# Four tiles of K ahead of the first V, and K's first half behind half of the weight fold, in a linear-attention and feed-forward kernel on eight cores

## The chip, the cores and the metric

The kernel runs on the 8 NeuronCores of one Trainium2 chip, each with 4 of the 32 sequences and no exchange between cores. The metric is the device time in microseconds of the slowest core.

## The reference

One layer on x of shape 32 x 2048 x 1024 in float32, cut to what matters:

```python
def attn(x):                      # 16 heads of 64
    Q, K, V = heads(x @ Wq.T + bq), heads(x @ Wk.T + bk), heads(x @ Wv.T + bv)
    Qf = relu(Q * 64**-0.25 @ P.T) + 1e-6
    Kf = relu(K * 64**-0.25 @ P.T) + 1e-6
    KV, Ksum = einsum('bhnf,bhnd->bhfd', Kf, V), Kf.sum(axis=2)
    out = einsum('bhnf,bhfd->bhnd', Qf, KV) / (einsum('bhnf,bhf->bhn', Qf, Ksum) + 1e-6)[..., None]
    return merge_heads(out) @ Wo.T + bo

def ffn(x):                       # 1024 -> 4096 -> 1024
    h = fix8(x @ w1 + b1)         # fix8 rounds to multiples of 2**-8
    h = fix8(piecewise_linear_gelu(h))
    return fix8(h @ w2 + b2)

x = x + layernorm(attn(layernorm(x)))
x = x + layernorm(ffn(layernorm(x)))
```

## The kernel before

A core's 4 sequences are 64 tiles of 128 rows. The first stage (the loop over `t`, line 778) reads each tile of x once. DVE takes its statistics (`ln_stats`, `ln_aggr`), POOL raises the variance to the power -1/2, DVE applies both (`ln_apply`, writes `xn`), PE transposes the tile in eight pieces (`ln_transpose`) and DVE copies the result out of PSUM into `xnT` (`ln_evac`); from tile 8 on a DMA transposes instead. Then `k_proj` (16 matmuls of 512 columns in two halves into banks 0 and 1, and after each half an add on DVE into `kf`), `k_floor` (the maximum with 1e-6 on DVE), `v_proj` (16 matmuls into banks 2 and 3, copied out by ACT into `vt`), and one tile later `kv_acc`, eight matmuls that add K'V into banks 5 to 7. From tile 3 on each step has two Q projections too (`q_proj`, evacuated by ACT, stored to DRAM).

The feature matrix P is folded into Wk and Wq on the chip. Wk comes in four pieces of 1 MB (`load_w`), each is cast to bf16, one half by DVE and one by ACT (`cast_w`), and `fold` multiplies it with P, 32 small matmuls for each half of the output columns, eight evacuations of 512 columns that ACT and DVE take in turn. The fold's first half needs pieces 0 and 1 alone, its second half pieces 2 and 3. Wv is cast and not folded. Wq is folded in the same way at t = 3, behind `v_proj(3)`, once it has been loaded into the place that Wk's float32 copy had.

All later stages (the chunks of M = KV Wo, the attention output, and the feed-forward part, by blocks of 256 rows) follow behind tile 63 and are not touched.

Order: nothing is scheduled by a tool. Each helper appends its instruction to the list of its engine, and an engine executes its list in the order in which the Python code ran; a helper's waits are semaphores that are worked out from the tokens (`t_...`) given to it. SP (`"Y"`) issues all loads of this stretch, in its written order too. Before the change SP issues: small constants, x tile 0, Wk in four pieces, x tile 1, Wv in four pieces, x tiles 2 and 3, then tiles 4 and 5 (each waits until `ln_apply` has read the tile four before it, whose buffer it takes), small constants, `sel`, and Wq in four pieces.

Work of the first tiles before the change, in the order of the text: LN and transposes of tile 0; fold of Wk, first and second half; statistics and apply of tile 1; `k_proj(0)`; transposes of tile 1; casts of Wv; `k_proj(1)`; `v_proj(0)`; floors; statistics of 2 and 3; apply of 2 and 3; transposes of 2; then for t = 1, 2, 3: `v_proj(t)`, statistics of t+4, apply of t+3, `kv_acc(t-1)`, transposes of t+2, with `k_proj(t)` at the head of each step from t = 2 on.

Lines that the steps name: casts L225 (DVE) and L226 (ACT), statistics L255 and L256, their aggregation L260, POOL's two L262 and L265, apply L271, transposes L283, evacuation L291, fold L311 with evacuations L318 (ACT) and L320 (DVE), K matmuls L371 and add L376, floor L383, V matmuls L389 and copy L394, Q matmuls L402, kv L421. DMAs have the line of the helper, L88.

Of the kernel before, what the change touches and what calls it, by code (L numbers as in the profile page):

```python
# [95 lines left out]
def build_program():  # L96
# [32 lines left out]
    with es:  # L129
# [4 lines left out]
        def sb(name, kb, cols, dt):  # L134
# [17 lines left out]
        xnT = [sb(f"xnT{i}", 148 + 8 * i, 8 * 512, BF16).rearrange("p (c j) -> p c j", j=512)  # L152
               for i in range(2)]
        kf = [sb(f"kf{i}", 164 + 2 * i, D, BF16) for i in range(2)]
        vt = [sb(f"vt{i}", 168 + 2080 * i / KB, 8 * 130, BF16).rearrange("p (c j) -> p c j", j=130)
              for i in range(2)]
        qst = [sb(f"qst{i}", 172.25 + i, 512, BF16) for i in range(4)]
# [71 lines left out]
            t_c0 = p.dma("Y", "c0", out, src)  # L229
        t_x[0] = p.dma("Y", "x0", xr[0], xtile[0])  # L230
        t_wk = [load_w("lk", k, wkf, wk_n) for k in range(4)]
        t_x[1] = p.dma("Y", "x1", xr[1], xtile[1])
        t_wv = [load_w("lv", k, wvf, wv_t) for k in range(4)]
        for t in range(2, 4):
            t_x[t] = p.dma("Y", f"x{t}", xr[t], xtile[t])

        t_one = p.V(lambda v: v.memset(one, 1.0))
        t_z = p.V(lambda v: v.memset(sel, 0.0))
        for col, val in ((c_half, -0.5), (c_q, 0.25), (c_seg, -31.5 / 64.0), (c_mag, MAGIC)):
            t_cst = p.V(lambda v, col=col, val=val: v.memset(col, val))  # L240
        for i in range(2):
# [34 lines left out]
        def load_x(t):  # L276
            t_x[t] = p.dma("Y", f"x{t % 4}", xr[t % 4], xtile[t], t_xn[t - 4])
# [27 lines left out]
        def fold(name, hf, src, dst, banks, t_src, ev):  # L305
            for d in range(8):
                n = hf * 8 + d
                i = banks[n % len(banks)]
                for c in range(4):
                    o = (hf * 4 + c) * D + d * 128  # L310
                    tt = p.T(lambda e, o=o, c=c, i=i: e.matmul(  # L311
                        bk[i][:, c * 128:c * 128 + 128], lhsT=src[:, o:o + 128], rhs=pbb,
                        start=(c == 0), stop=(c == 3)),
                        *((*t_src[4 * hf:4 * hf + 4], t_pbb, *t_free.get(i, ())) if c == 0 else ()),
                        sig=(c == 3))
                out = dst[:, d * D + hf * 512:d * D + hf * 512 + 512]
                if ev[n % len(ev)] == "S":
                    t_free[i] = [p.S(lambda s, out=out, i=i: s.copy(out=out, in_=bk[i]), tt)]  # L318
                else:
                    t_free[i] = [p.V(lambda v, out=out, i=i: v.tensor_copy(out=out, in_=bk[i]), tt)]  # L320
                t_fe[name] = [*t_fe.get(name, ())[-1:], *t_free[i]]
            return tt

        t_free = {}
# [17 lines left out]
        ln_evac(0)  # L342
        t_wkc += cast_w(2, stk, wkf, t_wk[2])
        fold("k", 0, stk, wkp, (0, 1, 2, 3), t_wkc, "SV")
        t_wkc += cast_w(3, stk, wkf, t_wk[3])
        t_fk = fold("k", 1, stk, wkp, (0, 1, 2, 3), t_wkc, "SV")
        ln_aggr(1, *ln_stats(1))
        ln_apply(1)
        for t in range(4, 6):
            load_x(t)  # L350
        for out, src in ((b1s, b1_d), (mskb, mskb_d), (msk16, msk16_d.rearrange("p (c j) -> p c j", j=16))):
            t_c1 = p.dma("Y", "c1", out, src)
        t_sel = p.dma("Y", "c2", sel[0:48], sel_d, t_z)
        t_wq = [load_w("lq", k, wqf, wq_n, *t_wkc[2 * k:2 * k + 2]) for k in range(4)]


        def centre_bo(t_in):
# [7 lines left out]

        t_ka, t_kf, t_ve, t_qe, t_kv, t_kve, t_qs = {}, {}, {}, {}, {}, {}, {}

        def k_proj(t):
            for hf in range(2):
                for d in range(8):  # L370
                    tt = p.T(lambda e, d=d, hf=hf: e.matmul(  # L371
                        bk[hf], lhsT=xnT[(t // 4) % 2][:, d, (t % 4) * 128:(t % 4) * 128 + 128],
                        rhs=wkp[:, d * D + hf * 512:d * D + hf * 512 + 512],
                        start=(d == 0), stop=(d == 7)),
                        *((t_te[t], *t_fe["k"], *t_free[hf]) if d == 0 else ()), sig=(d == 7))
                t_ka[(t, hf)] = p.V(lambda v, hf=hf: v.tensor_tensor(  # L376
                    out=kf[t % 2][:, hf * 512:hf * 512 + 512], in0=bk[hf],
                    in1=bkb[:, hf * 512:hf * 512 + 512], op=ALU.add),
                    tt, t_bkb, t_kv.get(t - 2))
                t_free[hf] = [t_ka[(t, hf)]]  # L380

        def k_floor(t):
            t_kf[t] = p.V(lambda v: v.tensor_scalar(out=kf[t % 2], in0=kf[t % 2], scalar1=EPS_ATT,  # L383
                                                    scalar2=None, op0=ALU.max), t_ka[(t, 1)])

        def v_proj(t):
# [11 lines left out]
        def q_proj(b, c):  # L398
            n = b * 8 + c
            bi = c % 2  # L400
            for d in range(8):
                tt = p.T(lambda e, d=d: e.matmul(  # L402
                    bk[bi], lhsT=wqp[:, d * D + c * 128:d * D + c * 128 + 128],
                    rhs=xnT[b % 2][:, d, :], start=(d == 0), stop=(d == 7)),
                    *((t_te[4 * b + 3], *t_free[bi], *t_fe["q"]) if d == 0 else ()), sig=(d == 7))
            t_qmm[b] = tt
            t_qe[n] = p.S(lambda s: s.activation(out=qst[n % 4], in_=bk[bi], func=AF.Relu,  # L407
                                                 bias=bqn[:, c:c + 1]), tt, t_bqe, t_qs.get(n - 4))
            t_free[bi] = [t_qe[n]]
# [6 lines left out]
        def kv_acc(t):  # L416
            s, u = divmod(t, 16)
            for c in range(8):
                b = bk[5 + c // 3]
                o = (c % 3) * 129  # L420
                tt = p.T(lambda e, c=c, b=b, o=o: e.matmul(  # L421
                    b[:, o:o + 129], lhsT=kf[t % 2][:, c * 128:c * 128 + 128],
                    rhs=vt[t % 2][:, c, 0:129], start=(u == 0 and c % 3 == 0),
                    stop=(u == 15 and c in (2, 5, 7))),
                    *((t_kf[t], t_ve[t], t_cst, t_bkb, *t_kve.get(s - 1, ())) if c == 0 else ()),
# [680 lines left out]
```

How the kernel before makes its waits and increments, by code:

```python
        def run(h):  # L64
            for s, v in (todo[:-1] if own else todo):
                h.wait_ge(s, v)
            ins = fn(h)
            if own and todo:
                ins.wait_op(todo[-1][0], todo[-1][1], "sem-ge")
            if sem is not None:
                ins.then_inc(sem, step)
# [18 lines left out]
    def done(self, eng, sig):  # L90
        n = self.count[sig]
        s = self.sem[sig]
        self.ops[eng].append(lambda h: h.wait_ge(s, n))
```

## Time and profile before

| what | us |
|---|---|
| time, median of 3 runs | 3126.4 |
| the three runs | 3126.4, 2863.38, 3311.34 |
| the profiled execution | 2864.24 |
| its span, slowest core (3) | 2862.7 |
| spans of the eight cores | 2856.7 to 2862.7 |
| PE busy | 2801.9 |
| DVE busy | 2063.2 |
| ACT busy | 1846.1 |
| POOL busy | 467.6 |

PE is TensorE (PEld its weight loads), DVE is VectorE, ACT is ScalarE, POOL is GpSimd, SP is SyncE. A row of a timeline gives the start, the time from the first to the last of the instructions merged in it, engine, line, operation, output and inputs, the count, and in brackets how long the engine had been idle and what ended that. A row of windows gives a stretch in us from the span's start, its length, the busy time of each engine with its instructions, the granted clock of TensorE as a share of 2.4 GHz, the busy share of the DMA engines and the rate. The first rows of a core's clock may stand at 1.00 for want of a record.

### The profile page before, as it was taken

Reading aid. Unit: us, or ns where it says so; the run is one execution under the profiler, and the core shown is the slowest. Engines: PE = TensorE matmul, PEld = TensorE weight load, DVE = VectorE, ACT = ScalarE, POOL = GpSimd, SP = SyncE. Lnnn points to the kernel's source line nnn. Section 1 sums busy time; section 2 is a strip of 40 time slices with the busy share of each in tenths; the row PEclk is TensorE's granted clock in tenths of the full one; section 3 lists DMA queues with packets and bytes.
Section 4 is the critical chain, followed back from the end, with each engine's and each line's share of the span. In section 5 each row is a group of like instructions: output and inputs, shape, how many; then the busy total and the mean of one; then the engine's idle time right before and its main releaser. Section 6 shows DMA issues by size and latency. Waiting matters only on the chain.

```text
span 2862.7 us, 47693 instructions; the slowest of 8 cores (2856.7 to 2862.7 us)
## 1 busy us (share of the span) xinstructions
PE 2801.9 (98%) x17762; PEld 1704.7 (60%) x17762; DVE 2063.2 (72%) x2657; ACT 1846.1 (64%) x2953; POOL 467.6 (16%) x1092
## 2 busy tenths in 40 slices
PE   6999999999889999999999999999999999999998
PEld 3444444444456666666666666666666666666665
DVE  5454344443378888788888888788888888878887
ACT  3222222222377787878777787878777788878776
POOL 0111111110001111211111111211111112212111
PEclk8999999999999999999999999999999999999999
DMA  8547999853445555565666556556665655555654
GB/s 261 137 102 130 156 146 160 157 125 85 150 142 177 177 177 174 178 196 184 189 193 182 177 177 197 178 174 182 185 201 180 198 185 163 178 177 179 192 181 147
DMA packets 287618, 488.91 MB, mean 171 GB/s; under 512 B 141424, under 2 KB 174320, under 8 KB 287392
## 3 DMA queue, kind: packets, MB, share of 16 engines
q1 hardware_dynamic: 278176, 469.08, 55.9%
q0 software_dynamic: 9216, 16.78, 5.2%
q8 instruction: 147, 2.41, 0.3%
q14 instruction: 79, 0.65, 0.1%
HBM read 412.90 MB, written 67.11 MB: 168 GB/s over the span
## 4 chain that ended last, share of the span: by engine, by line
PE 96%; DMA 1%; DVE 1%; ACT 1%; issue 0%; POOL 0%; SPq 0%; POOLq 0%; DVEq 0%; ACTq 0%
PE bk L668 31%; PE bk L726 30%; PE bk L371 8%; PE bk L585 8%; PE bk L389 8%; PE bk L402 7%; PE bk L538 1%; PE bk L421 1%; PE bk L554 1%; DMA wkf<-wk_n 1%; PE bk L479 0%; DMA qf<-qscr 0%; PE bk L311 0%; DMA xnF<-xn 0%; ACT stq L226 0%
## 5 line engine op out<-in xcount | busy, mean ns | idle before, releaser
L668 PE MATMUL bk<-xnF,w 128*128 128x256 bf16 x8192 | 937.2, 273 | 4.5 <-DMA xnF<-xn 1.3
L726 PE MATMUL bk<-w2r,yb 128*128 128x512 bf16 x4096 | 925.6, 379 | 0.0
L668 PEld LDWEIGHTS bk<-xnF,w 128*128 128x128 bf16 x8192 | 801.6, 98 | 146.5 <-issue 6.7
L681 ACT ACTIVATE kbuf<-bk,b1s 128x256 int32<-128x256 f32 x1024 | 426.5, 472 | 413.0 <-PE bk L668 413.0
L726 PEld LDWEIGHTS bk<-w2r,yb 128*128 128x128 bf16 x4096 | 398.3, 98 | 441.8 <-issue 6.5
L703 DVE TENSOR_TENSOR y1b<-y1b,y0b 128x1024 f32<-128x1024 f32 x256 | 312.4, 1220 | 152.5 <-ACT y1b L694 151.6
L394 ACT CAST vt<-bk 128x512 bf16<-128x512 f32 x128 | 75.1, 587 | 381.3 <-PE bk L389 381.3
L707 DVE TENSOR_TENSOR jbi<-jbi,y1b 128x1024 f32<-128x1024 int32 x256 | 313.5, 1225 | 8.8
L711 DVE SCALAR_TENSOR_TENSOR jbi<-jbi,y0b 128x1024 f32<-128x1024 f32 x256 | 313.0, 1223 | 5.5
L687 ACT ACTIVATE segb<-kbuf,cst 128x1024 int32<-128x1024 int32 x256 | 295.4, 1154 | 7.6 <-ACT kbuf L681 0.3
L694 ACT ACTIVATE y1b<-segb,cst 128x1024 f32<-128x1024 int32 x256 | 291.4, 1138 | 0.0
L692 ACT ACTIVATE y0b<-segb 128x1024 f32<-128x1024 int32 x256 | 270.1, 1055 | 12.1 <-ACT segb L687 0.4
L376 DVE TENSOR_TENSOR kf<-bk,bkb 128x512 bf16<-128x512 f32 x128 | 88.5, 692 | 228.3 <-PE bk L371 228.3
L371 PE MATMUL bk<-wkp,xnT 128*128 128x512 bf16 x1024 | 233.8, 382 | 2.5 <-DVE xnT L291 1.0
L585 PE MATMUL bk<-msb,qf 128*128 128x512 bf16 x1024 | 231.4, 379 | 2.3 <-ACT bk L573 2.3
L389 PE MATMUL bk<-wv,xnT 128*128 128x512 bf16 x1024 | 231.5, 379 | 2.2 <-DVE wv L225 2.2
L402 PE MATMUL bk<-xnT,wqp 128*128 128x512 bf16 x1024 | 231.8, 379 | 0.8 <-ACT wqp L318 0.8
L612 DVE SCALAR_TENSOR_TENSOR xr<-bk,st,xr 128x512 f32<-128x512 f32 x128 | 90.2, 747 | 148.3 <-POOL st L604 138.4
L716 DVE TENSOR_SCALAR yb<-jbi 128x1024 bf16<-128x1024 f32 x256 | 177.8, 695 | 20.8 <-PE bk L726 0.5
L698 DVE TENSOR_SCALAR jbi<-kbuf 128x1024 int32<-128x1024 int32 x256 | 177.7, 694 | 14.4 <-ACT kbuf L681 5.3
L750 POOL TENSOR_TENSOR st<-st 128x1 f32<-128x1 f32 x64 | 12.3, 193 | 1075.2 <-DVE rr L738 1075.2
L407 ACT ACTIVATE qst<-bk,bqn 128x512 bf16<-128x512 f32 x128 | 88.2, 689 | 148.2 <-PE bk L402 148.2
(110 smaller groups left out, 2313.9 us busy)
## 6 DMA issues: line engine op xcount, KB each, us to landing
w2r<-w2scr SPq DMA_DIRECT2D x512, 512.0 KB, 4.9
xr<-xin SPq DMA_DIRECT2D x128, 512.0 KB, 8.8
yout<-rr SPq DMA_DIRECT2D x64, 512.0 KB, 3.6
qscr<-qst SPq DMA_DIRECT2D x128, 128.0 KB, 6.0
qf<-qscr SPq DMA_DIRECT2D x32, 512.0 KB, 7.4
w<-w_d POOLq DMA_DIRECT2D x32, 256.0 KB, 7.1
mscr<-mst SPq DMA_DIRECT2D x32, 256.0 KB, 4.4
w2scr<-w_d POOLq DMA_DIRECT2D x32, 256.0 KB, 8.4
```

Source lines behind the costliest of these rows:

```text
L371: tt = p.T(lambda e, d=d, hf=hf: e.matmul(bk[hf], lhsT=xnT[(t // 4) % 2][:, d, (t % 4) * 128:(t % 4) * 128 + 128], rhs=wkp[:, d * D + hf * ...
L389: tt = p.T(lambda e, d=d, hf=hf: e.matmul(bk[2 + hf], lhsT=xnT[(t // 4) % 2][:, d, (t % 4) * 128:(t % 4) * 128 + 128], rhs=wv[:, d * D + h ...
L402: tt = p.T(lambda e, d=d: e.matmul(bk[bi], lhsT=wqp[:, d * D + c * 128:d * D + c * 128 + 128], rhs=xnT[b % 2][:, d, :], start=(d == 0), st ...
L585: tt = p.T(lambda e, c=c, b=b, hf=hf: e.matmul(b, lhsT=qf[J % 2][:, c, s2 * 128:s2 * 128 + 128], rhs=msb[:, c * D + hf * 512:c * D + hf * ...
L668: tt = p.T(lambda e, d=d, fc=fc, sub=sub: e.matmul(HB[a][:, sub * 256:sub * 256 + 256], lhsT=w1[:, d * FF + fc * 128:d * FF + fc * 128 + 1 ...
L681: t_k[(g, a)] = p.S(lambda s, sub=sub, fc=fc, o=o: s.activation(out=kbuf[g % 2][:, o:o + 256], in_=HB[a][:, sub * 256:sub * 256 + 256], fu ...
L687: t_seg[g] = p.S(lambda s: s.activation(out=segb, in_=kbuf[g % 2], func=AF.Identity, scale=1.0 / 64.0, bias=c_seg), t_k[(g, 1)], t_y1.get( ...
L694: t_y1[g] = p.S(lambda s: s.activation(out=y1b, in_=segb, func=AF.Gelu, scale=0.25, bias=c_q), t_p.get(g - 1))
L703: t_d[g] = p.V(lambda v: v.tensor_tensor(out=y1b, in0=y1b, in1=y0b[g % 2], op=ALU.subtract), t_y1[g])
L707: t_p[g] = p.V(lambda v: v.tensor_tensor(out=jbf, in0=jbi, in1=y1b, op=ALU.mult), t_d[g], t_j[g])
L711: t_z[g] = p.V(lambda v: v.scalar_tensor_tensor(out=jbf, in0=jbf, scalar=1.0 / 64.0, in1=y0b[g % 2], op0=ALU.mult, op1=ALU.add), t_p[g])
L726: tt = p.T(lambda e, f=f, pr=pr, n=n, s2=s2, hf=hf: e.matmul(ACC[n], lhsT=yb[q % 3][:, f * 256 + s2 * 128:f * 256 + s2 * 128 + 128], rhs=w ...
```

## The change

The tiles 1, 2 and 3 of x are loaded ahead of Wv. K's first half of tile 0 (`k_half(0, 0)`) stands between the two halves of the fold of Wk, and the second half of the fold takes its banks in the order 2, 3, 0, 1. Then a loop over t = 1, 2, 3 does statistics, apply, transposes, evacuation and K of each tile (with K's second half of tile 0 at t = 1), and the casts of Wv; K of tiles 2 and 3 goes into two more buffers, `kfx`. All four V projections come behind that loop. The loads of x tiles 4 and 5, three constants, `sel` and Wq are written behind it too. The wait for the fold's evacuations is kept for each half of the columns.

```diff
+        kfx = [sb(f"kfx{i}", 188.5 + 2 * i, D, BF16) for i in range(2)]
...
         t_wk = [load_w("lk", k, wkf, wk_n) for k in range(4)]
-        t_x[1] = p.dma("Y", "x1", xr[1], xtile[1])
+        for t in range(1, 4):
+            t_x[t] = p.dma("Y", f"x{t}", xr[t], xtile[t])
         t_wv = [load_w("lv", k, wvf, wv_t) for k in range(4)]
-        for t in range(2, 4):
-            t_x[t] = p.dma("Y", f"x{t}", xr[t], xtile[t])
...
-                t_fe[name] = [*t_fe.get(name, ())[-1:], *t_free[i]]
+                t_fe[(name, hf)] = [*t_fe.get((name, hf), ())[-1:], *t_free[i]]
...
         fold("k", 0, stk, wkp, (0, 1, 2, 3), t_wkc, "SV")
-        t_wkc += cast_w(3, stk, wkf, t_wk[3])
-        t_fk = fold("k", 1, stk, wkp, (0, 1, 2, 3), t_wkc, "SV")
-        ln_aggr(1, *ln_stats(1))
-        ln_apply(1)
-        for t in range(4, 6):
-            load_x(t)
-        for out, src in ((b1s, b1_d), (mskb, mskb_d), (msk16, msk16_d.rearrange("p (c j) -> p c j", j=16))):
-            t_c1 = p.dma("Y", "c1", out, src)
-        t_sel = p.dma("Y", "c2", sel[0:48], sel_d, t_z)
-        t_wq = [load_w("lq", k, wqf, wq_n, *t_wkc[2 * k:2 * k + 2]) for k in range(4)]
...
+        kfb = lambda t: kfx[t - 2] if t in (2, 3) else kf[t % 2]
+
+        def k_half(t, hf):
+            for d in range(8):
+                tt = p.T(lambda e, d=d: e.matmul(
+                    bk[hf], lhsT=xnT[(t // 4) % 2][:, d, (t % 4) * 128:(t % 4) * 128 + 128],
+                    rhs=wkp[:, d * D + hf * 512:d * D + hf * 512 + 512],
+                    start=(d == 0), stop=(d == 7)),
+                    *((t_te[t], *t_fe[("k", hf)], *t_free[hf]) if d == 0 else ()), sig=(d == 7))
+            t_ka[(t, hf)] = p.V(lambda v: v.tensor_tensor(
+                out=kfb(t)[:, hf * 512:hf * 512 + 512], in0=bk[hf],
+                in1=bkb[:, hf * 512:hf * 512 + 512], op=ALU.add),
+                tt, t_bkb, t_kv.get(t - 2))
+            t_free[hf] = [t_ka[(t, hf)]]
+
         def k_proj(t):
...
+            k_half(t, 0)
+            k_half(t, 1)
...
+        k_half(0, 0)
+        t_wkc += cast_w(3, stk, wkf, t_wk[3])
+        t_fk = fold("k", 1, stk, wkp, (2, 3, 0, 1), t_wkc, "SV")
+        for t in range(1, 4):
+            ln_aggr(t, *ln_stats(t))
+            ln_apply(t)
+            ln_transpose(t, t_te[t - 1])
+            ln_evac(t)
+            if t == 1:
+                k_half(0, 1)
+                k_floor(0)
+            k_proj(t)
+            k_floor(t)
+            if t == 1:
+                t_wvc = cast_w(0, wv, wvf, t_wv[0])
+            elif t == 2:
+                t_wvc += cast_w(1, wv, wvf, t_wv[1])
+        for k in (2, 3):
+            t_wvc += cast_w(k, wv, wvf, t_wv[k])
+        for t in range(4, 6):
+            load_x(t)
+        for out, src in ((b1s, b1_d), (mskb, mskb_d), (msk16, msk16_d.rearrange("p (c j) -> p c j", j=16))):
+            t_c1 = p.dma("Y", "c1", out, src)
+        t_sel = p.dma("Y", "c2", sel[0:48], sel_d, t_zs)
+        t_wq = [load_w("lq", k, wqf, wq_n, *t_wkc[2 * k:2 * k + 2]) for k in range(4)]
         t_wof = {}
         for t in range(NT):
             if t == 0:
-                k_proj(0)
-                ln_transpose(1, t_te[0])
-                ln_evac(1)
-                t_wvc = cast_w(0, wv, wvf, t_wv[0])
-                t_wvc += cast_w(1, wv, wvf, t_wv[1])
-                k_proj(1)
-                for k in (2, 3):
-                    t_wvc += cast_w(k, wv, wvf, t_wv[k])
                 v_proj(0)
-                k_floor(0)
-                k_floor(1)
-                for n in (2, 3):
-                    ln_aggr(n, *ln_stats(n))
-                for n in (2, 3):
-                    ln_apply(n)
-                ln_transpose(2, t_te[1])
-                ln_evac(2)
                 ln_aggr(4, *ln_stats(4))
                 load_x(6)
                 load_x(7)
                 continue
-            if t > 1:
+            if t > 3:
                 k_proj(t)
                 k_floor(t)
...
             kv_acc(t - 1)
-            if t + 2 < 8:
+            if 4 <= t + 2 < 8:
                 ln_transpose(t + 2, t_te[t + 1])
                 ln_evac(t + 2)
-            elif t + 2 < NT:
+            elif 8 <= t + 2 < NT:
                 ln_transpose_dma(t + 2)
```

## Rows read from the trace of the kernel before

**Rows 1.** The head of the page, and part 1, busy time by engine.
```profile
span 2862.7 us, 47693 instructions; the slowest of 8 cores (2856.7 to 2862.7 us)
PE 2801.9 (98%) x17762; PEld 1704.7 (60%) x17762; DVE 2063.2 (72%) x2657; ACT 1846.1 (64%) x2953; POOL 467.6 (16%) x1092
```

**Rows 2.** Part 2 of the page, PE's busy tenths in 40 slices.
```profile
PE   6999999999889999999999999999999999999998
```

**Rows 3.** Part 4 of the page, the chain that ended last, by engine.
```profile
PE 96%; DMA 1%; DVE 1%; ACT 1%; issue 0%; POOL 0%; SPq 0%; POOLq 0%; DVEq 0%; ACTq 0%
```

**Rows 4.** Windows of core 3, the start and the change of stage.
```profile
0.00:76.00 76.00, 51.33 (x333) 30.95 (x334) 46.66 (x88) 26.80 (x37) 6.70 (x18) 0.87 0.78 246
...
760.00:800.00 40.00, 23.33 (x145) 13.60 (x144) 15.51 (x24) 16.52 (x31) 4.05 (x14) 0.87 0.47 149
```

**Rows 5.** Timeline of core 3, PE, 24 to 76 us.
```profile
24.70 3.57 PE L311 MATMUL bk<-pbb,stk 128*128 128x128 bf16 x32 [1.59 <-DVE stk L225]
29.15 6.02 PE L371 MATMUL bk<-wkp,xnT 128*128 128x512 bf16 x16 [0.88 <-DVE wkp L320]
...
36.64 3.61 PE L371 MATMUL bk<-wkp,xnT 128*128 128x512 bf16 x16 [1.03 <-DVE xnT L291]
42.44 3.61 PE L389 MATMUL bk<-wv,xnT 128*128 128x512 bf16 x16 [2.19 <-DVE wv L225]
...
50.41 0.63 PE L421 MATMUL bk<-vt,kf 128*128 128x129 bf16 x8
50.88 0.61 PE L283 MATMUL bk<-idb,xn 128*128 128x128 bf16 x8
51.32 3.62 PE L371 MATMUL bk<-wkp,xnT 128*128 128x512 bf16 x16
...
62.60 3.62 PE L389 MATMUL bk<-wv,xnT 128*128 128x512 bf16 x16
...
75.37 3.61 PE L402 MATMUL bk<-xnT,wqp 128*128 128x512 bf16 x16 [0.77 <-ACT wqp L318]
```

**Rows 6.** Timeline of core 3, DVE, 23 to 43 us.
```profile
23.16 0.69 DVE L320 CAST wkp<-bk 128x512 bf16<-128x512 f32 x1 [0.16 <-PE bk L311]
...
23.76 0.68 DVE L225 CAST stk<-wkf 128x1024 bf16<-128x1024 f32 x1
...
28.92 0.69 DVE L255 BATCH_NORM_STATS2 st<-xr 128x6 f32<-128x512 f32 x1
...
31.38 0.81 DVE L271 TENSOR_SCALAR xn<-xr,mv,rsA 128x1024 bf16<-128x1024 f32 x1 [0.95 <-POOL rsA L265]
...
35.81 0.68 DVE L291 COPY xnT<-bk 128x1024 bf16<-128x1024 bf16 x1
...
40.29 0.69 DVE L376 TENSOR_TENSOR kf<-bk,bkb 128x512 bf16<-128x512 f32 x1 [1.03 <-PE bk L371]
40.90 1.28 DVE L225 CAST wv<-wvf 128x1024 bf16<-128x1024 f32 x2
42.10 0.76 DVE L383 TENSOR_SCALAR kf<-kf 128x1024 bf16<-128x1024 bf16 x2
```

**Rows 7.** Windows of core 3, 29 to 34 and 35 to 41 us.
```profile
29.00:34.00 5.00, 4.85 (x12) 1.75 (x13) 2.91 (x6) 1.46 (x2) 0.74 (x2) 0.50 1.01 311
35.00:41.00 6.00, 4.23 (x25) 1.92 (x23) 3.89 (x7) 1.52 (x2) 0.00 (x0) 1.00 0.99 337
```

**Rows 8.** Timeline of core 0, PE, the first V projection.
```profile
41.18 3.31 PE L389 MATMUL bk<-wv,xnT 128*128 128x512 bf16 x10 [2.19 <-DVE wv L225]
44.71 1.76 PE L389 MATMUL bk<-wv,xnT 128*128 128x512 bf16 x5 [0.22 <-issue]
```

**Rows 9.** Window of core 0, 43 to 45 us.
```profile
43.00:45.00 2.00, 1.78 (x5) 0.76 (x5) 1.97 (x5) 0.58 (x1) 1.23 (x3) 0.50 0.93 321
```

**Rows 10.** The tile wqf, core 3: its loads' issue and landing.
```profile
L88 SPq DMA_DIRECT2D wqf<-wq_n x4: 496/898/2497, 35.7 to 39.9; - x4
...
DMA to landing us min/median/max: 12.5/16.2/18.3
```

More of the change, by code:

```diff
@@ L231, in build_program @@
         t_wk = [load_w("lk", k, wkf, wk_n) for k in range(4)]
-        t_x[1] = p.dma("Y", "x1", xr[1], xtile[1])
+        for t in range(1, 4):
+            t_x[t] = p.dma("Y", f"x{t}", xr[t], xtile[t])
         t_wv = [load_w("lv", k, wvf, wv_t) for k in range(4)]
-        for t in range(2, 4):
-            t_x[t] = p.dma("Y", f"x{t}", xr[t], xtile[t])
         t_one = p.V(lambda v: v.memset(one, 1.0))
-        t_z = p.V(lambda v: v.memset(sel, 0.0))
+        t_zs = p.V(lambda v: v.memset(sel, 0.0))
         for col, val in ((c_half, -0.5), (c_q, 0.25), (c_seg, -31.5 / 64.0), (c_mag, MAGIC)):
@@ L366, in build_program @@
         t_ka, t_kf, t_ve, t_qe, t_kv, t_kve, t_qs = {}, {}, {}, {}, {}, {}, {}
-        def k_proj(t):
[L369 to L380, printed above, removed]
+        kfb = lambda t: kfx[t - 2] if t in (2, 3) else kf[t % 2]
[11 more added lines that the diff above has]
+            t_free[hf] = [t_ka[(t, hf)]]
+        def k_proj(t):
+            k_half(t, 0)
+            k_half(t, 1)
         def k_floor(t):
-            t_kf[t] = p.V(lambda v: v.tensor_scalar(out=kf[t % 2], in0=kf[t % 2], scalar1=EPS_ATT,
+            t_kf[t] = p.V(lambda v: v.tensor_scalar(out=kfb(t), in0=kfb(t), scalar1=EPS_ATT,
                                                     scalar2=None, op0=ALU.max), t_ka[(t, 1)])
@@ L404, in q_proj @@
                     rhs=xnT[b % 2][:, d, :], start=(d == 0), stop=(d == 7)),
-                    *((t_te[4 * b + 3], *t_free[bi], *t_fe["q"]) if d == 0 else ()), sig=(d == 7))
+                    *((t_te[4 * b + 3], *t_free[bi], *t_fe[("q", 0)], *t_fe[("q", 1)]) if d == 0 else ()), sig=(d == 7))
             t_qmm[b] = tt
@@ L421, in kv_acc @@
                 tt = p.T(lambda e, c=c, b=b, o=o: e.matmul(
-                    b[:, o:o + 129], lhsT=kf[t % 2][:, c * 128:c * 128 + 128],
+                    b[:, o:o + 129], lhsT=kfb(t)[:, c * 128:c * 128 + 128],
                     rhs=vt[t % 2][:, c, 0:129], start=(u == 0 and c % 3 == 0),
```

## The prediction

> **What bounds the kernel now.** I read the page first: a span of 2862.7 us on core 3, in which PE is busy 2801.9 us [rows 1]. The sum below is made against the profiled execution itself, 2864.24 us, which is the span and 1.5 us around it. The median of the three runs shown is 3126.4 us and their lowest 2863.38; the profiled execution is as quick as the lowest, so my number is for executions like it and says nothing of the 260 us by which the others lie above. The slices show PE at 9 tenths nearly everywhere, with one dip in the very first and a small one near the tenth and eleventh [rows 2]. The chain that ended last is 96% PE [rows 3]. So whatever delays PE at the start is not taken back later, unless a later wait of PE hangs on something other than PE's own progress. The windows by stage say where PE idles: 24.7 of the first 76 us, and 16.7 of the 40 us at the change from attention to the feed-forward part [rows 4]. That later idle time waits for things that PE's own last projections start (stored Q read back, the chunks of M), so it moves along with PE. The change touches only the first 76 us, and the measure of it is one event: when the last V projection of the first four tiles ends (62.60+3.62 = 66.2 now [rows 5]). From there on both kernels issue the same work in the same order: the fold of Wq, then the first Q projection at 75.37.
>
> **The order of the work in this stretch.** Before, tile 1's normalisation is written to DVE right behind the second half of the fold, ahead of K(0); its transposes are ready while K(0) runs, and K(1) follows at 36.64 [rows 5]. After, the loop over t = 1 to 3 writes for each tile: statistics, apply, transposes, evacuation, K(t) with its two adds, the floor, and a cast of Wv. DVE runs in its written order, and so statistics of tile 2 stand behind the adds of K(1), which wait for K(1)'s matmuls; K(2) in turn waits for tile 2's transposes. Nothing else is given to PE in between, since all V projections are now behind K(3). That makes one closed ring per tile: PE works, then DVE, POOL, DVE, PE (transposes), DVE, and PE again.
>
> **Step 1, K's first half behind half of the fold.** The last evacuation of the fold's first half ends at 23.16+0.69 = 23.85 [rows 6]. K(0)'s first half starts 0.14 later, at 24.0, and takes 3.6 us (half of the 6.02 of K(0) at the lower clock, with its drain [rows 5]), to 27.6. Its add is written to DVE ahead of DVE's half of the last Wk cast, which before started at 23.76 [rows 6]. The add costs 0.61 (pitch from 40.29 to 40.90), the cast 0.68, PE's start behind it 0.26 (24.44 to 24.70): the second half of the fold starts at 29.15 instead of 24.70, 4.45 us late, and ends at 32.7. The work put in that gap was worth 3.4 us of PE time, so step 1 itself is a small loss of about 1 us. Queued behind the waiting add are the cast, the fold's evacuations on DVE and tile 1's statistics; all shift.
>
> **Step 2, tile 1.** Before, the fold ended at 28.27 and the apply of tile 1 at 31.38+0.81 = 32.19, or 3.92 us later [rows 6]; K(0) hid this. Now only K(0)'s second half is left, and it is written behind tile 1's transposes, so nothing hides it: apply ends at 36.6, the transposes start at 36.8, and PE idles 4.1 us. Then come 8 transposes (0.61) and 24 matmuls of 512 columns, K(0)'s half and K(1). At 3.45 us for 16 (the pitch in the run from 51.32 on, where kv and transposes together take 0.91 [rows 5]) K(1) ends at 42.7.
>
> **Step 3, the ring for tiles 2 and 3.** From the end of K(t-1): add 0.65 (40.25 to 40.90), floor 0.34 (0.67 for two), cast of Wv 0.60, statistics to the end of the apply 3.27 (28.92 to 32.19, POOL's power in it), transposes 0.15+0.61, evacuation 0.04+0.68 and PE's start 0.15 (35.81+0.68 to 36.64) [rows 5, 6]. Sum 6.5 us, in which PE does 0.6. K(t) itself takes 3.6. So a tile costs 10.1 where before K, transposes and everything else of PE stood back to back.
> With the full clock: K(1) ends 42.7, K(2) 52.8, K(3) 62.9. V(0) waits for K(3)'s add, the floor and two casts on DVE (0.65+0.34+1.20+0.26 = 2.45; Wv landed long ago, below) and starts at 65.4, against 42.44 before. Behind it stand V(0) to V(3), kv twice and one set of transposes, 4 x 3.45 + 0.91 + 0.47 = 15.2 with 0.15 of drain: V(3) ends at 80.7, +14.5 us.
>
> **Step 4, the clock.** K(0) took 6.02 us because the granted clock was 0.50 from 29 to 34 us, the lower of the two levels (1.2 GHz); from 35 on it was 1.00 [rows 7]. It had come up some 5 us after PE began to work without large pauses (29.15 to 34). On core 0 a pause of about 2.2 us ahead of V(0) was enough for the clock to fall again: V(0) began at 41.18 and ended at 46.47, 5.3 us in place of 3.6 [rows 8], and the window in its middle stands at 0.50 [rows 9]. Core 3 kept its clock over a pause of 2.19 [rows 5]. The new pauses are 4.1 and twice 6.5 us. So I take each of the three bursts (K(0)'s half with K(1), K(2), K(3)) to begin at the lower clock and to stay there 5 us: the first ends at 36.8+1.0 for the transposes +4.0 (9.4 matmuls at 0.43) + 14.6 x 0.216 = 45.0; K(2) starts 6.7 later and takes 5.0+0.9+0.2, to 57.8; K(3) from 64.5 to 70.6; V(0) at 73.1. For V(0), behind a pause of 2.45, I take 0.8, half of core 0's loss. V(3) ends at 73.1+15.4+0.8, about 89.2: +23 us. Ends: +14.5 if the clock never falls, +31 if it stays low from 36.8 until V(0) is through (K(1) to 48.1, each ring 6.9 and each K 7.0, V(0) 3.4 more: 97.1).
> The Trainium skill has a rule on this (TensorE: Matmul & The Clock Gate, section HAM oscillation — how this bites in real kernels): matmul bursts with a wait between them start cold each time. By that rule the sum is the +23 or more; a clock that holds over the pauses gives +14.5. Core 0's row agrees with the rule and core 3's pause of 2.19 neither way; the same page's Part 4 says that transposes don't count as work for the gate, which no row here shows.
>
> **Step 5, the transfers.** x2 and x3 (1 MB) pass ahead of Wv, and at 337 GB/s [rows 7] that makes Wv 3.1 us later. Before, DVE's last Wv casts ran at 40.90 [rows 6], so Wv is there by 44 at the latest; the last casts are asked for at 70 (65 at least at the full clock). Nothing. Tiles 1 to 3 (1.5 MB, 4.7 us) land behind Wk, whose last cast ran at 23.76, so by 28.5, and the first is read at 33. The loads of x4 and x5, three small constants, sel and the four pieces of Wq are written to SP behind the loop now; SP's only wait there is tile 1's apply (36.6 in place of 32.2), so Wq goes out about 4.5 us later: issued by 44.4, landed up to 18.3 us later [rows 10], 63, and first cast on ACT behind V(3) at 81 or later. Nothing. If this cover went, it would cost its own lateness, below zero excluded as ACT casts Wq behind V(3) in both. Two more K buffers and the split of the fold's wait by halves cost no instruction and nothing.
> Ahead of the Q projection stand in both kernels ACT's four casts of Wq, behind V(3)'s evacuation, and the fold: 66.2 to 75.37. DVE's casts come earlier now, but ACT's set the end, so 9.1 us stay. No PE time is saved that could pay back: the pauses that go are 1.0, 2.2 and 0.5 us around K(1) and V(0), and they are in the sums above, since I compare end with end.
>
> **Sum.** 2864.2 + 23 = 2887 us, 0.8% slower.
>
> **Rivals.**
> (a) The ring as above, but the clock holds: +14.5, 2879. For it: core 3 over 2.19 us. Against: the pauses are two to three times as long.
> (b) The ring with the clock low all through: +31, 2895. For it: 16 matmuls at the lower clock last 6.8 us, little more than the 5 us after which core 3's clock came up; against: it did come up within such a burst on both cores [rows 5, 8].
> (c) The other side: the normalisation of tiles 1 to 3 hides beside the projections, as x is there early. Place: DVE between the adds. Price: the pauses of 1.0+2.2+0.5 around K(1) and V(0) go, and K(0), begun early, pulls the clock up before the fold's end, 2.4 (6.02 to 3.61): up to -6, 2858. It decides at one point: tile 2's statistics must begin before K(1)'s add. DVE's written order speaks against it.
> (d) The change doesn't tell: the start grows as forecast but is absorbed, because the idle 17 us at 760 to 800 [rows 4] end at a time not set by PE. Then 2864. Against: the weights of the feed-forward part are loaded in step with the tiles, and what is awaited there is made by the last Q projections.
>
> **Chances.** Forecast (2881 to 2893) 0.55, (a) 0.16, (b) 0.10, (c) 0.05, (d) 0.05, the rest 0.09 for what lies between or beside them, such as a chip whose executions differ by some 0.2%. Range 2874 to 2898: from under (a), since the same kernel scatters by a few us from one execution to the next, to over (b); it leaves out (c), (d) and part of the rest. A measurement of this kernel tells about 2%, 57 us, from no change. All cases lie within: within 2% 0.97, slower 0.02, faster 0.01.
>
> **What would show it.** Right: PE idle of 4 us ahead of tile 1's transposes; two PE pauses of about 6.5 us ahead of K(2) and K(3), put down to DVE's evacuation of the transposes and to the apply; tile 2's statistics right behind a Wv cast; clock 0.5 at the starts of K(1), K(2) and K(3); V(0) near 73 and the first Q projection near 98; the stage from 76 on unchanged in length. Wrong: V(0) before 60, or a first Q projection late but a span that isn't, which would be (d), or a wait for Wv or Wq by ACT or DVE behind 60 us.

## The result, and the profile after

The changed kernel takes 2889.7 us (median of five runs), the kernel before 2863.84 (median of five, the three of the table and two more). Their ratio is 1.0084, with a 95% interval of 1.006 to 1.0107: slower by 0.84%, less than the 2% that count as a difference. I had forecast 2887, 0.8% slower than the profiled 2864.24; set beside the table's median of 3126.4 the same number would read as a gain, which it was not meant to be. Times far above the rest, like the table's 3126.4 and 3311.34, are left out of every ratio here; in the changed kernel's own such time, 3460.98, the four cores of one die had a granted clock of 0.81 where the others had 0.99.

The head of the page after, with the chain that ended last by engine, answers to [rows 1, 3]:

```profile
span 2887.5 us, 47696 instructions; the slowest of 8 cores (2879.6 to 2887.5 us)
...
PE 2811.1 (97%) x17762; PEld 1707.3 (59%) x17762; DVE 2063.3 (71%) x2657; ACT 1841.9 (64%) x2953; POOL 466.5 (16%) x1092
...
PE 94%; DMA 3%; DVE 1%; ACT 1%; issue 0%; SPq 0%; POOL 0%; POOLq 0%; DVEq 0%; ACTq 0%
```

PE does the same 17762 matmuls and is busy 9.2 us longer, though nothing was added for it: that is the lower clock, as the windows below show. The span grew by 24.8, so some 15.6 us are waiting. The windows (stretch, length, busy time by engine, granted clock, DMA share, GB/s), of core 2, the slowest now, show where [rows 4]:

```profile
0.00:76.00 76.00, 40.27 (x190) 21.52 (x191) 36.57 (x71) 14.26 (x18) 4.92 (x16) 0.75 0.72 225
76.00:100.00 24.00, 19.92 (x149) 11.81 (x148) 11.38 (x21) 12.42 (x20) 1.36 (x4) 0.93 0.23 67
100.00:400.00 300.00, 300.00 (x1579) 143.89 (x1578) 134.10 (x237) 74.92 (x120) 45.12 (x82) 1.00 0.71 135
```

In the first 76 us PE is busy 40.3 instead of 51.3 and issues 190 matmuls instead of 333, at a mean clock of 0.75. From 100 to 400 us it never stops. The timeline of PE on core 2, up to the first Q projection, answers to [rows 5] (V projections are L384 now, K L362, Q L397):

```profile
24.47 3.33 PE L362 MATMUL bk<-wkp,xnT 128*128 128x512 bf16 x8 [0.88 <-DVE wkp L320]
29.39 2.46 PE L311 MATMUL bk<-pbb,stk 128*128 128x128 bf16 x32 [1.58 <-DVE stk L226]
35.92 1.01 PE L283 MATMUL bk<-idb,xn 128*128 128x128 bf16 x8 [4.07 <-DVE xn L271]
36.72 7.50 PE L362 MATMUL bk<-wkp,xnT 128*128 128x512 bf16 x24
49.36 1.01 PE L283 MATMUL bk<-idb,xn 128*128 128x128 bf16 x8 [5.13 <-DVE xn L271]
51.24 5.32 PE L362 MATMUL bk<-wkp,xnT 128*128 128x512 bf16 x16 [0.88 <-DVE xnT L291]
61.69 1.01 PE L283 MATMUL bk<-idb,xn 128*128 128x128 bf16 x8 [5.13 <-DVE xn L271]
63.58 5.97 PE L362 MATMUL bk<-wkp,xnT 128*128 128x512 bf16 x16 [0.88 <-DVE xnT L291]
72.09 8.59 PE L384 MATMUL bk<-wv,xnT 128*128 128x512 bf16 x32 [2.54 <-DVE wv L226]
...
85.36 3.62 PE L384 MATMUL bk<-wv,xnT 128*128 128x512 bf16 x16
...
98.69 3.61 PE L397 MATMUL bk<-xnT,wqp 128*128 128x512 bf16 x16 [0.77 <-ACT wqp L318]
```

The brackets are the waits: 4.07 ahead of tile 1's transposes, 5.13 ahead of those of tile 2 and again of tile 3, each of these two with 0.88 more for the copy out of PSUM, and 2.54 ahead of V(0). DVE between K(1) and K(2) shows the ring (one row each for add, floor, cast, the two halves of the statistics, apply and copy) [rows 6]:

```profile
44.26 0.69 DVE L367 TENSOR_TENSOR kf<-bk,bkb 128x512 bf16<-128x512 f32 x1 [1.04 <-PE bk L362]
44.99 0.43 DVE L378 TENSOR_SCALAR kf<-kf 128x1024 bf16<-128x1024 bf16 x1
45.33 0.69 DVE L226 CAST wv<-wvf 128x1024 bf16<-128x1024 f32 x1
45.93 0.69 DVE L255 BATCH_NORM_STATS2 st<-xr 128x6 f32<-128x512 f32 x1
46.53 0.68 DVE L256 BATCH_NORM_STATS2 st<-xr 128x6 f32<-128x512 f32 x1
...
48.40 0.81 DVE L271 TENSOR_SCALAR xn<-xr,mv,rsA 128x1024 bf16<-128x1024 f32 x1 [0.94 <-POOL rsA L265]
...
50.40 0.69 DVE L291 COPY xnT<-bk 128x1024 bf16<-128x1024 bf16 x1 [1.19 <-PE bk L283]
```

No row of the statistics waits for x tile 2's transfer; DVE took the tile up only at 45.93, because K(1)'s adds, a floor and a cast were written ahead of it. Windows of the same core around the bursts; the granted clock is the number behind POOL's count [rows 7]:

```profile
29.00:32.00 3.00, 2.37 (x32) 1.85 (x32) 2.10 (x5) 2.12 (x5) 0.00 (x0) 1.00 1.04 345
36.00:41.00 5.00, 5.00 (x19) 2.25 (x19) 1.31 (x2) 1.11 (x2) 0.00 (x0) 0.50 1.00 342
41.00:44.00 3.00, 3.00 (x15) 1.31 (x13) 1.19 (x3) 0.98 (x1) 0.00 (x0) 0.99 0.89 273
51.00:56.00 5.00, 4.76 (x15) 1.83 (x16) 0.78 (x2) 0.00 (x0) 0.00 (x0) 0.63 0.97 334
63.00:69.00 6.00, 5.42 (x15) 1.99 (x16) 1.13 (x2) 0.00 (x0) 0.00 (x0) 0.55 0.24 81
```

On this core the clock was full in the fold, fell to 0.50 over the pause of 4 us, came back at 41, and did the same around each later burst.

The start of the first Q projection is a good measure of this stretch, since both kernels do the same from there. Averaged over the eight cores of one profiled execution it moved from 74.35 us (71.96 to 76.89) to 98.56 (96.63 to 100.50), by 24.2. The experiments are read by this mean and by the time. The mean has a scatter of its own: in the run with Wq's casts early, below, the code up to V(0) is that of the kernel before, and yet V(0) starts at 39.7 us on average instead of 40.4. A difference under 1 us says nothing by itself.

### The profile page after: what moved, and what is told of

Same layout as the page of the kernel before. It is cut to its first block, busy times and chain, and to the rows that moved or that the text cites. A ratio compares the mean times of both kernels' runs of the same rounds, so it can differ in the third digit from the quotient of the medians.

```text
span 2887.5 us, 47696 instructions; the slowest of 8 cores (2879.6 to 2887.5 us)
## 1 busy us (share of the span) xinstructions
PE 2811.1 (97%) x17762; PEld 1707.3 (59%) x17762; DVE 2063.3 (71%) x2657; ACT 1841.9 (64%) x2953; POOL 466.5 (16%) x1092
## 4 chain that ended last, share of the span: by engine, by line
PE 94%; DMA 3%; DVE 1%; ACT 1%; issue 0%; SPq 0%; POOL 0%; POOLq 0%; DVEq 0%; ACTq 0%
PE bk L663 31%; PE bk L721 30%; PE bk L362 8%; PE bk L580 8%; PE bk L384 7%; PE bk L397 7%; PE bk L533 1%; DMA xnT<-xn 1%; PE bk L416 1%; PE bk L549 1%; DMA wkf<-wk_n 1%; DMA qscr<-qst 0%; SPq L88 0%; PE bk L474 0%; DMA qf<-qscr 0%
## 5 line engine op out<-in xcount | busy, mean ns | idle before, releaser
L362 PE MATMUL bk<-wkp,xnT 128*128 128x512 bf16 x1024 | 239.1, 388 | 4.3 <-DVE xnT L291 1.8
L384 PE MATMUL bk<-wv,xnT 128*128 128x512 bf16 x1024 | 232.8, 381 | 2.5 <-DVE wv L226 2.5
L397 PE MATMUL bk<-xnT,wqp 128*128 128x512 bf16 x1024 | 231.8, 379 | 0.8 <-ACT wqp L318 0.8
```

Source lines behind the costliest of these rows:

```text
L362: tt = p.T(lambda e, d=d: e.matmul(bk[hf], lhsT=xnT[(t // 4) % 2][:, d, (t % 4) * 128:(t % 4) * 128 + 128], rhs=wkp[:, d * D + hf * 512:d ...
L384: tt = p.T(lambda e, d=d, hf=hf: e.matmul(bk[2 + hf], lhsT=xnT[(t // 4) % 2][:, d, (t % 4) * 128:(t % 4) * 128 + 128], rhs=wv[:, d * D + h ...
L397: tt = p.T(lambda e, d=d: e.matmul(bk[bi], lhsT=wqp[:, d * D + c * 128:d * D + c * 128 + 128], rhs=xnT[b % 2][:, d, :], start=(d == 0), st ...
```

## The experiments

Nine runs, on two chips. On the second, used for the last five, the kernel before itself took 2891 to 2892 us (median), so ratios and the starts of the first Q projection are compared, not times across chips. All starts are set beside the two traces read above; neither kernel was traced again. Each time is within 2% of the kernel before, so none counts as faster or slower by itself; the argument rests on the traces, and the intervals say how far the times bear it out.

**Is it the order on DVE?** Statistics and apply of the next tile are written ahead of K(t):

```diff
+        ln_aggr(1, *ln_stats(1))
+        ln_apply(1)
         for t in range(1, 4):
-            ln_aggr(t, *ln_stats(t))
-            ln_apply(t)
             ln_transpose(t, t_te[t - 1])
             ln_evac(t)
+            if t < 3:
+                ln_aggr(t + 1, *ln_stats(t + 1))
+                ln_apply(t + 1)
```

> The changed kernel with one thing moved: statistics and apply of tile t+1 are written to DVE ahead of K(t)'s adds, not behind them. Theory (the ring DVE-POOL-DVE-PE-DVE behind K(t)'s adds is what costs, and the lower clock comes out of its pauses): the PE pauses of 5.1 and 0.9 us ahead of K(2) and K(3) shrink to some 2.4 in all (add, floor, cast, evacuation), V(0) comes at about 59 to 61 instead of 72.1, and the time falls by 10 to 14 us from the changed kernel's, to about 2877. Rival (what costs is the transfers, x ahead of Wv and Wq behind the loop): nothing moves, V(0) stays at 70 or later. Rival (the pauses matter little, the loss is K(0)'s half and its late second fold): V(0) earlier by 2 us at most.

Measured: 2876.86 us against 2865.69 of before, ratio 1.0032 (1.0019 to 1.0045). V(0) starts at 58.9 on average (71.8 in the changed kernel), the first Q projection at 84.5, 14.0 earlier. PE's waits from 34 to 76 us on its slowest core (7), and two rows of its timeline:

```profile
PE bk L362 <- DVE xnT L291: 4.2, 2, 2.1
PE bk L283 <- DVE xn L271: 4.1, 1, 4.1
PE bk L384 <- DVE wv L226: 2.5, 1, 2.5
...
46.83 3.61 PE L362 MATMUL bk<-wkp,xnT 128*128 128x512 bf16 x16 [2.09 <-DVE xnT L291]
50.28 0.61 PE L283 MATMUL bk<-idb,xn 128*128 128x128 bf16 x8
```

The two waits of 5.13 for the apply are gone, two of 2.09 for the copy are left, and K(2) takes 3.61: on this core the clock held. It didn't everywhere: K(2) began at the lower clock on two cores of eight (5.30 us), K(3), behind pauses of 2.1 to 2.4 us, on five. The order on DVE made 14 of the 24 us, the clock that came back with it counted in. Both rivals fall as the main cause, since neither the transfers nor K(0)'s half were touched. What is left, some 10 us, is the wait of 4.07 ahead of tile 1 with the low clock behind it, the two waits of 2.09 and the one of 2.54 ahead of V(0).

**How much of it is the clock?** Idle work on PE in the pauses, nothing else:

```diff
+        def warm(n):
+            for i in range(n):
+                p.T(lambda e: e.matmul(bk[7], lhsT=idb, rhs=wkp[:, 0:512], start=True, stop=True),
+                    *((t_bqe, *t_fe[("k", 1)]) if i == 0 else ()))
...
         for t in range(1, 4):
+            warm(15 if t == 1 else 20)
             ln_aggr(t, *ln_stats(t))
...
             t_wvc += cast_w(k, wv, wvf, t_wv[k])
+        warm(9)
```

> The changed kernel with idle work on PE in its pauses: 15 matmuls of 512 columns into an unused bank ahead of tile 1's transposes, 20 each ahead of those of tiles 2 and 3, 9 ahead of V(0); nothing waits for them but what is queued on PE. It asks how much of the loss is the lower clock and how much is waiting. Theory: the waits stay, the clock holds; K(2) and K(3) take 3.6 us each in place of 5.3 and 6.0, the first burst 5.3 in place of 7.5, V(0) 3.6 in place of 5.1: the first Q projection about 9 us earlier (near 90), the time near 2880, 9 below the changed kernel's and 15 above that of before. Rival (the clock is only a symptom, the ring alone makes all): within 3 us of the changed kernel, since what bursts save is waited for elsewhere. Rival (clock is most of it): within 5 us of the kernel before.

Measured: 2879.04 us, ratio 1.0038 (1.0022 to 1.0054); the first Q projection at 88.7, 9.8 us earlier than in the changed kernel and 14.4 later than before. From the timeline of PE, core 1 (L777 is the idle work):

```profile
34.19 5.34 PE L362 MATMUL bk<-wkp,xnT 128*128 128x512 bf16 x24
39.37 4.48 PE L777 MATMUL bk<-wkp,idb 128*128 128x512 bf16 x20
44.66 0.61 PE L283 MATMUL bk<-idb,xn 128*128 128x128 bf16 x8 [0.82 <-DVE xn L271]
46.14 3.61 PE L362 MATMUL bk<-wkp,xnT 128*128 128x512 bf16 x16 [0.87 <-DVE xnT L291]
```

On all eight cores the first burst took 5.34 us and K(2) and K(3) 3.61. So the 24.2 us split into about 14.4 of waiting and 9.8 of a lower clock that the waiting brought on. The split holds to about 1 us, as the means do. More work on PE made the kernel faster: PE wasn't short of time but of something to do. It doesn't give back the waiting, though, and both rivals fall.

**Is it the transfers?** The kernel before, with the tiles 1 to 3 of x ahead of Wv:

```diff
-        t_x[1] = p.dma("Y", "x1", xr[1], xtile[1])
+        for t in range(1, 4):
+            t_x[t] = p.dma("Y", f"x{t}", xr[t], xtile[t])
         t_wv = [load_w("lv", k, wvf, wv_t) for k in range(4)]
-        for t in range(2, 4):
-            t_x[t] = p.dma("Y", f"x{t}", xr[t], xtile[t])
```

> The kernel before with the new order of the loads alone: x tiles 1 to 3 ahead of Wv. Theory: Wv lands about 3 us later, at 41, just when DVE asks for its last piece (40.9); V(0) moves by 0 to 1 us, the time by less than 1 us. Rival (the transfers are to blame): V(0) 3 us or more later and the time up by more than 3 us.

Measured: ratio 0.9997 (0.9987 to 1.0007), the first Q projection at 75.1, +0.7, which is within the scatter. The trace shows more than the mean. V(0) waits for ACT's last Wv cast on six of eight cores, and that cast for the landing of Wv (core 4; ACT's row first, then PE's):

```profile
39.14 1.04 ACT L226 CAST wv<-wvf 128x1024 bf16<-128x1024 f32 x1 [1.86 <-DMA wvf<-wv_t]
...
40.33 5.30 PE L388 MATMUL bk<-wv,xnT 128*128 128x512 bf16 x16 [3.48 <-ACT wv L226]
```

On five cores the wait ahead of V(0) is 3.3 to 4.1 us in place of 2.19, and on six the clock was low in V(0), which took 5.30 us instead of 3.61. That V(0) still starts at 40.35 us on average, as before (40.4), is in part chance: K(1) started 1.0 us earlier in this execution (33.6 against 34.6), since the clock was up in K(0) on more of the cores. So in the old order the new order of the loads costs something like 1 us. That is small beside 24, and the rival, 3 us or more, falls. This run leaves Wq's loads where they were; for these see below.

**K's first half behind half of the fold, alone** (the split with its waits by halves, in the order of the kernel before):

```diff
+        k_half(0, 0)
         t_wkc += cast_w(3, stk, wkf, t_wk[3])
-        t_fk = fold("k", 1, stk, wkp, (0, 1, 2, 3), t_wkc, "SV")
+        t_fk = fold("k", 1, stk, wkp, (2, 3, 0, 1), t_wkc, "SV")
...
             if t == 0:
-                k_proj(0)
+                k_half(0, 1)
```

> The kernel before with step 1 alone: K(0)'s first half between the halves of the fold, its add ahead of DVE's last Wk cast. Theory: the second half of the fold starts 4.4 us later, tile 1's statistics too, and K(0)'s second half hides part of them; K(1) starts 1 to 2 us later than in the kernel before, and the time rises by 1 to 2 us, most of it on cores whose clock comes up late. Rival (filling the pause pays, as PE works where it stood): K(1) starts as early as before or up to 2 us earlier.

Measured: ratio 1.0 (0.9989 to 1.0011); K(1) starts at 36.6 on average against 34.6, V(0) at 42.5 against 40.4, the first Q projection at 76.3, +1.9. That is the expected size, too small for the time to show.

**The new loop without that half:**

```diff
-        k_half(0, 0)
         t_wkc += cast_w(3, stk, wkf, t_wk[3])
-        t_fk = fold("k", 1, stk, wkp, (2, 3, 0, 1), t_wkc, "SV")
+        t_fk = fold("k", 1, stk, wkp, (0, 1, 2, 3), t_wkc, "SV")
+        ln_aggr(1, *ln_stats(1))
+        ln_apply(1)
+        k_proj(0)
         for t in range(1, 4):
-            ln_aggr(t, *ln_stats(t))
-            ln_apply(t)
+            if t > 1:
+                ln_aggr(t, *ln_stats(t))
+                ln_apply(t)
...
             if t == 1:
-                k_half(0, 1)
                 k_floor(0)
```

> The changed kernel with step 1 undone: the whole fold first, tile 1's statistics and apply written ahead of K(0)'s adds as in the kernel before, K(0) behind the fold, then the new loop. With the run of step 1 alone it splits the loss in two. Theory: tile 1's normalisation is hidden beside K(0) again, K(1) starts near 36 as before, the rings for tiles 2 and 3 stay; V(0) 3 to 5 us earlier than in the changed kernel, at 67 to 69, the time 2884 to 2887. Rival (step 1 is harmless in the new kernel too, as alone): V(0) within 1 us of the changed kernel's 72.

Measured: ratio 1.0047 (1.0015 to 1.008). K(1) starts at 32.3 to 33.5, V(0) at 65.1, 6.7 us before the changed kernel, the first Q projection at 92.6, 5.9 before it. More than the 3 to 5 I expected. The two waits of 5.13 are still there, at the lower clock:

```profile
33.03 3.61 PE L362 MATMUL bk<-wkp,xnT 128*128 128x512 bf16 x16 [1.19 <-DVE xnT L291]
41.78 1.01 PE L283 MATMUL bk<-idb,xn 128*128 128x128 bf16 x8 [5.13 <-DVE xn L271]
```

So the halved K(0) costs 1.9 us in the old order, where its second half still covers most of tile 1's normalisation, and 5.9 in the new one, where that half is written behind the transposes and a pause of 4 us opens, with the clock lost over it. The loop makes the other 18 of the 24 us.

Both shares have a catch: this run keeps the wait for the fold's evacuations by halves, so K(0) starts right behind the fold, where the kernel before idles 0.88 us [rows 5]. Core 5 (no bracket, no wait):

```profile
24.07 3.57 PE L311 MATMUL bk<-pbb,stk 128*128 128x128 bf16 x32 [1.59 <-DVE stk L226]
27.43 4.00 PE L362 MATMUL bk<-wkp,xnT 128*128 128x512 bf16 x16
```

K(1) starts at 32.9 on average here and at 34.6 in the kernel before. So up to 1.7 of the 5.9 us may be this gain, which the changed kernel makes no use of, and then the loop's rings cost that much more. No run has the split of the wait alone; it is an open chance to make the kernel before faster.

**A version that reaches the Q projections sooner than both.** What both kernels have is a pause of 2.66 us or more ahead of Wq's fold, for ACT's casts of Wq (in the kernel before, for DVE's on cores 1, 5 and 6, with 2.66 to 3.43 us), and in the kernel before there are 2.19 us ahead of V(0) for DVE's casts of Wv. Both are matters of written order, so casts were moved up in the kernel before. First those of Wq, ahead of V(3):

```diff
+            if t == 3:
+                t_wqc = [x for k in range(4) for x in cast_w(k, stq, wqf, t_wq[k])]
             v_proj(t)
             if t == 3:
-                t_wqc = [x for k in range(4) for x in cast_w(k, stq, wqf, t_wq[k])]
```

> The kernel before with the casts of Wq written ahead of V(3), so that ACT makes them before V(3)'s copies and not behind them. It aims at the pause of 2.6 us ahead of Wq's fold, which both kernels have. Theory (ACT's casts set the start of the fold, Wq has long landed): the fold starts right behind V(3), the first Q projection comes 2 to 3 us earlier, the time falls by 2 to 4 us. Rival (the evacuations of the fold set its end whenever it starts, or Wq lands too late and holds V(3)'s copies): no gain or a loss of 1 to 3 us.

Measured: the first Q projection at 70.6, 3.8 us earlier than before, 0.7 of it there already at V(0), ahead of anything that was moved; ratio 0.999 (0.9961 to 1.0019), which doesn't tell it from no change. Then, in addition, the last two casts of Wv ahead of K(1):

```diff
-                k_proj(1)
                 for k in (2, 3):
                     t_wvc += cast_w(k, wv, wvf, t_wv[k])
+                k_proj(1)
                 v_proj(0)
```

> As the run before it, and the last two pieces of Wv are cast ahead of K(1)'s adds on DVE, not behind them, so that V(0) follows K(1) without the pause of 2.2 us. Theory: Wv's last piece lands about when K(1)'s first half ends, the pause shrinks to 0.5 or less, the first Q projection comes 4 to 5 us earlier than in the kernel before, the time falls by 4 to 6 us to about 2860 on this chip. Rival (Wv's landing sets the end, DVE waits for it with K's adds behind it): K(1)'s adds are late, V(0) gains less than 1 us over the run before it.

Measured: V(0) 1.6 us earlier than in the run before it (38.1 against 39.7), the first Q projection at 70.9, nothing gained. Ratio 0.9979 (0.9954 to 1.0003). Where did the earlier V(0) go? DVE and PE of core 2:

```profile
59.42 0.69 DVE L255 BATCH_NORM_STATS2 st<-xr 128x6 f32<-128x512 f32 x1 [7.37 <-DMA xr<-xin]
...
63.80 2.49 DVE L225 CAST stq<-wqf 128x1024 bf16<-128x1024 f32 x4
...
65.35 1.05 PE L311 MATMUL bk<-pbb,stq 128*128 128x128 bf16 x16 [3.21 <-DVE stq L225]
```

DVE stood 7.37 us at the statistics of tile 6, whose x is queued behind the 4 MB of Wq, with DVE's Wq casts written behind it. That transfer lands at about the same time whatever PE has done: these statistics begin at 57.6 to 59.4 us on the eight cores here and at 58.7 to 60.0 in the kernel before, where DVE waits 3.3 to 7.6 us for them too. A gain ahead of it ends there. Writing the casts of Wq at t = 2, ahead of that wait, should free it:

```diff
-            if t == 3:
-                t_wqc = [x for k in range(4) for x in cast_w(k, stq, wqf, t_wq[k])]
             v_proj(t)
+            if t == 2:
+                t_wqc = [x for k in range(4) for x in cast_w(k, stq, wqf, t_wq[k])]
```

> As the last version (Wq's and Wv's casts early), but the casts of Wq are written at t = 2, behind V(2) and ahead of DVE's statistics of tile 6, which in the run before waited 7.4 us on core 2 for x tile 6, queued behind the 4 MB of Wq, with DVE's Wq casts behind them. Theory (that wait of DVE, at 59 us whatever PE has done, is why the earlier V(0) of the last version gained nothing): the casts are done by about 60, the fold starts right behind V(3) at 62 to 63 instead of 65.4, the first Q projection comes near 68, 6 to 7 us earlier than in the kernel before, and the time is 5 to 8 us below it. Rival (the transfers of Wq and x set the end of this stage, not the order of the casts): the first Q projection stays near 70.5.

> The last version once more, beside the run with the casts at t = 2, since its interval (0.9954 to 1.0003) left open whether it gains. Theory: 3 to 4 us below the kernel before, ratio 0.9985 to 0.999. Rival: nothing, within 1 us.

Measured on one chip: the casts at t = 2 give 0.9977 (0.9957 to 0.9998), the last version again 0.9981 (0.9967 to 0.9996). The first Q projection comes at 68.6 and 70.5; before, 74.35. The fold starts right behind V(3), with 0.3 us of wait in place of 2.66 (core 4):

```profile
59.48 0.69 DVE L255 BATCH_NORM_STATS2 st<-xr 128x6 f32<-128x512 f32 x1 [1.51 <-DMA xr<-xin]
...
63.13 1.32 PE L311 MATMUL bk<-pbb,stq 128*128 128x128 bf16 x16 [0.31 <-DVE kf L376]
```

The statistics of tile 6 still begin at 59.48, the barrier is unmoved, but nothing hangs on it now. This version is 5.8 us earlier at the first Q projection than the kernel before and 30 earlier than the changed one. By the time the gain is 0.2%: both intervals lie just below 1, while the first measurement of the last version (0.9954 to 1.0003) did not. Which of the two is the better the times can't say, only the trace.

## Why the prediction came out as it did, and which steps failed

The steps, on the slowest core, forecast and measured. They were made from core 3 and measured on core 2, which accounts for some tenths in each start.

| step | forecast | measured |
|---|---|---|
| second half of the fold starts | 29.15 | 29.39 |
| transposes of tile 1 | 36.8 | 35.92 |
| K(1) ends | 45.0 | 44.2 |
| pause K(1) to K(2), with transposes | 6.7 | 7.0 |
| K(2), K(3) take | 6.1, 6.1 | 5.3, 6.0 |
| V(0) starts | 73.1 | 72.1 |
| V(3) ends | 89.2 | 89.0 |
| first Q projection | near 98 | 98.7 |

**What failed, in short.** The ring and the lower clock came as forecast. The step that failed is step 1, the price of K's first half behind half of the fold. I had put it at a loss of about 1 us; it measured 1.9 by itself and 5.9 in the new loop. The sum came out all the same, since I had counted the pause that this step opens under step 2. The base of the sum was weak too. 2887 is +23 on the 2864.24 us of one profiled execution; beside 3126.4, the median of the three runs that I had, it would be a gain of 239 us. That 2864 was the right time to start from was an assumption. The two further runs of the kernel before (2863.84 and 2863.15) bore it out, and against that base the change is +0.84%, with 0.8% forecast.

**Step 1.** I had booked the pause of 4.1 us in step 2, as if it were the loop's, while the run without the half shows that it belongs to the two together. A second part of it was mis-sized: I took 3.57 us for the fold's second half, and it took 2.46 on core 2, as K's half ahead of it had kept PE at work and the clock was already full there. That is a gain of 1.1 us which I left out. It came on three of eight cores only; the others took 3.2 to 3.6 us. It was lost at once, as the clock fell again over the next 4 us. The split of the fold's wait by halves, which I put at nothing, is worth nothing in the changed kernel, but up to 1.7 us where the whole of K(0) stands behind the fold.

**Steps 2 and 3, the ring,** carried the sum and held. The pause is 5.13 + 1.01 + 0.88 = 7.0; the sum of rows gave 6.5 at the full clock and I took 6.7; with the transposes at the lower clock (1.01 in place of 0.61) it should have been 6.9. That the ring is a matter of order was shown by moving only the order (14.0 us back), not argued.

**Step 4, the clock,** was right in kind. Its size was +8.5 us in the forecast (23 less 14.5) and 9.8 in the run with filled pauses, two fifths of the loss. V(0) lost about 1.5 us to the clock where I had put 0.8: V(0) and V(1) together took 8.59 us, against 7.07 on core 1, where the clock held. That V(3) ends within 0.2 us of the forecast is in part luck: K(2) was 0.8 us quicker than forecast and V(0) 0.7 slower.

The Trainium skill has the rule (TensorE: Matmul & The Clock Gate, section HAM oscillation — how this bites in real kernels) that bursts with waits between them start cold each time; by it the forecast was +23 or more. The windows above agree behind the long pauses: 0.50 at 36 us, 0.63 and 0.55 over the later bursts. Behind the pauses of 2.09 us in the run with the order changed, K(2) began at the lower clock on two cores of eight only, so for short pauses it isn't each time.

**Step 5, the transfers.** In the changed kernel they cost nothing that a row shows. On core 2 the last of Wv is there when ACT's last cast of it starts, at 40.9, and V(0) comes at 72; Wq goes out from 38.8 to 40.4 and lands up to 17.7 us later, and its first cast is at 86.2. In the old order, x ahead of Wv was felt on five cores (above), by way of a later Wv and of the clock, but the time didn't show it (0.9997).

**The rivals.** (a) and (b), the clock holding or low throughout, gave 2879 and 2895. The run with filled pauses makes (a) real: the first Q projection came 14.4 us later than before, against its +14.5. By the ratio of 1.0038 the time rose by some 11 us only, so that it reads 2879.04 on its chip is in part chance. (c), the normalisation hidden beside the projections, was to be decided by whether tile 2's statistics begin before K(1)'s add: they began at 45.93, behind the add at 44.26. (d), a later wait that absorbs the loss, falls. That wait, for the stored Q read back at the change of stage, was 7.83 us on core 3 before and is now, on core 2:

```profile
820.12 1.87 PE L533 MATMUL bk<-qf,ksz 128*16 128x256 bf16 x8 [9.24 <-DMA qf<-qscr]
```

It is 6.7 to 9.7 us on the eight cores before and 7.2 to 10.4 after, 0.7 more on average. It didn't shrink; whether it grew, one execution of each kernel can't say. On average over the cores the first Q projection moved by 24.2 us and the span by 23.8, so the stages behind it kept their length, as forecast.

## What to carry to other kernels

Loading data earlier helps only if the engine that reads it first comes to it earlier: find the instruction that stands ahead of that reader in its engine's order, and what that one waits for. Where one engine serves both the input of the next tile and the output of this one, write the next tile's input first, and keep PE's independent work (here V projections) between the two ends of such a ring, as the kernel before does. A gain ahead of a transfer that lands at a fixed time ends at that transfer, so look for what is written behind its reader and doesn't need it.

## What the runs showed of the hardware that was not expected

The granted clock fell over pauses of about 2 us on some cores and not on others. Over 2.19 us ahead of V(0) it fell on one core of eight in the kernel before [rows 8, 9] and on three of eight in the run with K's half alone; over 2.19 to 4.06 us on six of eight in the run with the order of the loads, where one core kept it over 3.29; over 2.09 us ahead of K(2) on two of eight in the run with the order on DVE. A pause of PE can thus cost more than its length: V(0) took 5.30 us in place of 3.61. And 64 matmuls of 512 columns whose results nobody reads, put in the pauses (64 x 0.216 = 13.8 us of PE), brought the first Q projection 9.8 us forward.
